# Norms of q and k: from a token-wise product with reductions to ones products on squares of the slot-wise q and k

## The chip, the cores and the metric

The kernel runs on one core of one Trainium2 chip. The metric is the device time of one execution in microseconds (us); its median over several runs is compared. PE is the matrix engine (TensorE), DVE is VectorE, ACT is ScalarE, POOL is GpSimd, and SP issues most DMAs.

## The reference, cut to what matters

The layer is attention, mixture of experts, a small local attention and the experts again, each on a layer norm and with a residual. The change lies in the first part and in the hand-over from it to the first expert unit.

```python
q = split_heads(tokens @ Wq, 16)            # 8 batches, 16 heads, 256 tokens, 16 wide
k, v = kv[..., :16], kv[..., 16:]           # v is 64 wide
q, k, v = l2norm(q), l2norm(k), l2norm(v)
attn = jnp.square(jax.nn.relu(jnp.einsum('bhid,bhjd->bhij', q, k)))
out = tanh_norm(jnp.einsum('bhij,bhjd->bhid', attn, v))
x = x + out @ Wout
x = x + ffn(_layernorm(x))                  # 32 experts, top 8, and a shared one
```

The norms of q and k are not applied to q and k. Scores are taken unnormalised; the factor 1/|k|^2 goes with 1/|v| into v, and 1/|q|^2 goes into the factors of the output.

## The kernel before, in words

Each engine runs a list of instructions in the order in which it is written, and semaphores tie the lists together. Three banks of PSUM (5, 6 and 7) are given out in turns by a table (`attention_turns`); a job waits until the job three turns ahead of it has freed its bank.

**A pass over batch b.** The attention works in 32 steps: 8 batches b of 4 groups g of 4 heads. For each step PE makes scores (`score`, PS<-qk, 8 matmuls), ACT takes their relu in two halves (L583, rl), DVE multiplies scores and relu in two halves (L896, aT), PE multiplies by v (`attend`, PS<-aT,v), and ACT copies and squares the output (L590 and L593). Into these steps are written the products for the next batch n = b+1 and the late work of q = b-1 and r = b-2. A product is written as three matmuls of a high and a low part (`split3`):

- `pairs(n, t)`: q and k of all heads by token (PS<-wah,xTh and two more, 128x512). It serves the norms alone. ACT squares it (L570, sqqk), DVE sums over 16 columns (L880), takes a floor (L886) and a reciprocal (L888, rr).
- `group(n, j)`: q and k again, laid out in slots of 32 rows for the scores, six matmuls of 128x256 (PS<-xTh,wah and so on). A slot holds the q of a head in one half and zeros in the other. Slots j=0 and j=2 hold q, j=1 holds k.
- `values(n, t, k)`: v by token, three matmuls of 128x512 each.
- `norms(q)`: sums over the squares of the attention output by a matmul with ones in the right rows (PS<-sqO,ind, 8 matmuls into four sets of 32 output partitions); `keep_norms` (ACT, n2T), `transpose_norms` (PE) and `gather_norms` (DVE, n2o) bring them to tokens.

**POOL in a pass.** `inverse_deviation` (L409, L411), then for q the root of the output norms (L438, sr, a power) and its product (L442), then for each half of n's tokens a power (L425, vi), a product (L428) and the scaling of v (L434). `attend` of the next batch waits for the last of these.

**Weights of the experts.** 32 pieces of 128x196 come through six stages (wfs). ACT makes the high part (L613), DVE the low part (L941), and piece k may be loaded when the low part of piece k-6 is done. ACT takes 4 pieces a batch, in batches 0 to 7, one at the end of each step. The same SP queue issues these loads and, behind them, the expert weights of tokens (L361 writes them to memory, L375 spreads them into wbc).

**Hand-over.** Unit u=0 of the experts has 17 pairs p (gate and up product on PE, SiLU on ACT, L1115 and L1120 on DVE, high part on ACT, low part on POOL, down product on PE). The end of the attention of batches 6 and 7 is written between its pairs: `spread_factors` (PS<-FT,sel), `norms`, `project`, `output_factors` (L908 to L924), `scale_output` (L931).

## Time and profile before

| | |
|---|---|
| median of 3 runs | 548.19 us (547.99 to 548.92) |
| the profiled execution, its own time | 546.98 us, span 545.2 us |
| PE busy | 526.1 us (96% of the span) |
| DVE, ACT, POOL busy | 421.7, 371.2, 332.5 us |
| first expert product on PE | 214.83 us |

The durations of the trace come from the profiled execution; its time is 1.21 us below the median. The matmuls' ends are modelled and overlap in the trace (a 128x512 matmul is shown with 0.39 us and the next starts 0.23 us later), so work on PE is read from start to start, not from the durations.

### The profile page before, as it was taken

The page shows a single profiled execution, that of the slowest core. Times are in us where ns is not written, and L with a number is a line of the kernel's source. Part 1 is how long each engine was busy: PE and PEld are TensorE (multiplying, and loading weights), DVE is VectorE, ACT ScalarE, POOL GpSimd, SP SyncE. Part 2 cuts the span into 40 slices and gives each one's busy share as a digit, 9 for nine tenths or more (in the row PEclk, how much of TensorE's full clock was granted, in tenths as well). Part 3 has the DMA queues.
Part 4 walks back from the last instruction along what each step waited for, and adds up shares of the span by engine and source line. Part 5 has one row for each costly group of instructions (what it writes and reads, how often), then busy time and mean ns, then how long its engine had stood idle before and what let it go on. Part 6 is the DMA issues. An engine that isn't in the chain of part 4 may idle for free.

```text
span 545.2 us, 10298 instructions
## 1 busy us (share of the span) xinstructions
PE 526.1 (96%) x3322; PEld 394.0 (72%) x3322; DVE 421.7 (77%) x1004; ACT 371.2 (68%) x682; POOL 332.5 (61%) x282
## 2 busy tenths in 40 slices
PE   7899899999999999998999999999999999999997
PEld 6565667676666666776778778778778877788884
DVE  5877888788979687669679679779778778777765
ACT  5697877686778876654555965965965965755654
POOL 6754938475865664484566656656655655666562
PEclk9999999999999999999999999999999999999999
DMA  7401010101010100850490940850860870761930
GB/s 222 131 2 31 1 32 1 32 0 32 1 31 1 31 2 21 189 122 1 107 208 7 222 116 5 207 132 6 197 141 7 194 163 5 181 149 42 220 74 20
DMA packets 37254, 44.77 MB, mean 82 GB/s; under 512 B 5840, under 2 KB 20304, under 8 KB 37200
## 3 DMA queue, kind: packets, MB, share of 16 engines
q1 hardware_dynamic: 32512, 42.40, 33.3%
q10 hardware_dynamic: 4688, 1.71, 1.3%
q8 instruction: 27, 0.44, 0.4%
q14 instruction: 27, 0.22, 0.2%
HBM read 40.94 MB, written 3.15 MB: 81 GB/s over the span
## 4 chain that ended last, share of the span: by engine, by line
PE 29%; POOL 12%; issue 9%; DVE 1%; DMA 1%; ACT 0%; POOLq 0%; DVEq 0%; SPq 0%; ACTq 0%
PE PS L1247 28%; POOL hl L519 10%; DMA wbc<-w_dram 1%; POOL mrstd L510 1%; POOL rstd L463 1%; DVE OTs L931 0%; PE PS L1534 0%; PE PS L1368 0%; DVE PS L1115 0%; DVE wsel L991 0%; POOL fxl L470 0%; PE PS L1555 0%; DVE hb L1120 0%; POOL mve L507 0%; DVE hl L1233 0%
## 5 line engine op out<-in xcount | busy, mean ns | idle before, releaser
L519 POOL TENSOR_TENSOR hl<-hb,hh 128x512 fp32r<-128x512 f32 x127 | 164.5, 1296 | 128.7 <-ACT hh L737 125.5
L730 ACT ACTIVATE sil<-PS 128x512 f32<-128x512 f32 (+1 forms) x136 | 80.8, 595 | 78.8 <-PE PS L1247 77.6
L1115 DVE TENSOR_TENSOR PS<-sil,PS 128x512 f32<-128x512 f32 x128 | 88.3, 690 | 53.0 <-PE PS L1247 32.3
L1247 PE MATMUL PS<-fxh,wfh 128*128 128x512 f32 x264 | 105.1, 398 | 2.5 <-DVE hb L1120 2.5
L737 ACT ACTIVATE hh<-hb 128x512 fp32r<-128x512 f32 x128 | 80.3, 627 | 35.1 <-DVE hb L1120 34.3
L1247 PE MATMUL PS<-fxl,wfh 128*128 128x512 f32 x264 | 104.2, 395 | 0.0
L1247 PE MATMUL PS<-fxh,wfl 128*128 128x512 f32 x264 | 103.8, 393 | 0.0
L1120 DVE TENSOR_TENSOR hb<-PS,wbc 128x512 f32<-128x512 f32 x128 | 88.5, 691 | 13.7 <-DMA wbc<-w_dram 6.4
L896 DVE SCALAR_TENSOR_TENSOR aT<-PS,rl 128x1024 f32<-128x1024 f32 x64 | 75.2, 1217 | 15.0 <-ACT rl L583 14.7
L583 ACT ACTIVATE rl<-PS 128x1024 f32<-128x1024 f32 x64 | 62.9, 1051 | 18.7 <-PE PS L1247 18.7
L438 POOL TENSOR_TENSOR sr<-n2o,half 128x32 f32<-128x32 f32 x7 | 37.9, 5413 | 44.3 <-DVE n2o L903 44.3
L1247 PE MATMUL PS<-aT,v 128*64 128x256 f32 x512 | 62.3, 385 | 0.6 <-POOL v L434 0.6
L1247 PEld LDWEIGHTS PS<-fxh,wfh 128*128 128x128 f32 x264 | 49.6, 188 | 15.8 <-DVE hb L1120 3.4
L1247 PEld LDWEIGHTS PS<-fxh,wfl 128*128 128x128 f32 x264 | 49.6, 188 | 11.9
L1247 PEld LDWEIGHTS PS<-fxl,wfh 128*128 128x128 f32 x264 | 49.6, 188 | 11.4
L1247 PE MATMUL PS<-hh,wfh 128*128 128x512 f32 x128 | 54.2, 424 | 1.0 <-DVE hl L1233 0.6
L1247 PE MATMUL PS<-hh,wfl 128*128 128x512 f32 x128 | 50.6, 396 | 0.0
L1247 PE MATMUL PS<-hl,wfh 128*128 128x512 f32 x128 | 50.5, 394 | 0.0
L1247 PEld LDWEIGHTS PS<-aT,v 128*64 128x64 f32 x512 | 34.0, 136 | 22.6 <-issue 5.6
L425 POOL TENSOR_TENSOR vi<-nm,half 128x16 f32<-128x16 f32 x14 | 40.5, 2894 | 9.8 <-DVE rr L888 9.8
L1247 PE MATMUL PS<-qk 32*128 32x256 f32 x512 | 37.5, 398 | 4.0 <-DVE aT L896 3.3
L1247 PEld LDWEIGHTS PS<-qk 32*128 32x128 f32 x512 | 24.4, 184 | 11.2 <-issue 7.1
(186 smaller groups left out, 899.6 us busy)
## 6 DMA issues: line engine op xcount, KB each, us to landing
wbc<-w_dram SPq DMA_DIRECT2D x48, 512.0 KB, 11.5
wbc<-w_dram SPq DMA_DIRECT2D x32, 128.0 KB, 3.0
wbc<-w_dram SPq DMA_DIRECT2D x16, 256.0 KB, 4.2
wfs<-wf_dram SPq DMA_DIRECT2D x32, 98.0 KB, 2.3
band_dram<-zero SPq DMA_DIRECT2D x16, 80.0 KB, 1.7
band<-band_dram ACTq DMA_DIRECT2D x4, 320.0 KB, 3.0
X<-x_dram SPq DMA_DIRECT2D x1, 896.0 KB, 8.0
Osb<-wa_dram SPq DMA_DIRECT2D x3, 256.0 KB, 3.8
```

What stands on the lines that cost most here:

```text
L425: g.tensor_tensor(vi[:, t, :], nm[:, n % 3, t, 2 * H:3 * H], half[:, 1:2].to_broadcast([P, H]), ALU.pow).then_inc(A("vi"), 1)
L438: g.tensor_tensor(sr[:, :, :], n2o[:, :, :], half[:, 0:1].unsqueeze(2).to_broadcast([P, 2, H]), ALU.pow).then_inc(A("sr"), 1)
L463: g.tensor_tensor(rstd[:, :], ve[:, :], half[:, 1:2].to_broadcast([P, CT]), ALU.pow).then_inc(F("p_rstd"), 1)
L510: g.tensor_tensor(mrstd[:, :], mve[:, :], half[:, 1:2].to_broadcast([P, CT]), ALU.pow).then_inc(M("m_rstd"), 1)
L519: g.tensor_tensor(hl[:, n % RING, :], hb[:, n % RING, :], hh[:, n % RING, :].bitcast(F32), ALU.subtract).then_inc(F("hl"), 1)
L583: s.activation(rl[:, f, :, :], PS[:, S0 + 2 * f:S0 + 2 * f + 2, :], ACT.Relu).then_inc(A("relu"), 1)
L730: s.activation(sil[0:rows, n % 2, :], PS[0:rows, G0 + n % 2, :], ACT.Silu).then_inc(F("silu"), 1)
L737: s.activation(hh[:, n % RING, :], hb[:, n % RING, :], ACT.Copy).then_inc(F("hh"), 1)
L896: v_.scalar_tensor_tensor(aT[:, i % 2, 2 * f:2 * f + 2, :], PS[:, S0 + 2 * f:S0 + 2 * f + 2, :], 0.0, rl[:, f, :, :], ALU.max, ALU.mult).t ...
L1115: v_.tensor_tensor(PS[:, bank, :], sil[:, n % 2, :], PS[:, bank, :], ALU.mult).then_inc(F("t"), 1)
L1120: v_.tensor_tensor(hb[:, n % RING, :], PS[:, bank, :], wbc[u % 2][:, p, :], ALU.mult).then_inc(F("h"), 1)
L1247: return nc.tensor.matmul(o, w, m, start=start, stop=stop)
```

## The change

The token-wise product of q and k (`pairs`), its squares and its reductions go, and with them 512 columns of `wa`. In their place:

- POOL adds the two halves of each q slot (zeros in one of them) and squares the sum (`square_queries`, two adds and two products of 128x256 a batch); ACT squares the k slots (`square_keys`, 128x512). For batch 0 DVE does both.
- PE sums over 16 rows by four matmuls with ones (`pair_sums`, PS<-sqq,indp and PS<-sqk,indp, 128x256 in, 32 partitions out), added into the bank in which the sums of the output squares (`output_sums`) already lie. One copy, one transposition and one reciprocal for both halves then serve q, k and output. `qk` is held twice.
- The order in a pass is new: the three `group` products come first, then `output_sums`, and the four `values` products come in two pairs.
- In batch 0 the second scores are written in halves (`score_half`), and fewer idle-filling transpositions stand there (4 and 4 for 6 and 10).
- Weight pieces: 8 stages, taken by the table `PIECES_IN_SLOTS` (none in batches 0 and 7, 4 in 1 and 6, 6 in 2 to 5).
- ACT runs a SiLU on one column at the very start, and the loads at the start are cut differently (`in_x1`, `in_wq0`, `in_wq1`).
- In unit 0 of the experts the late attention work of batch 7 stands one to two pairs earlier.

```diff
-FIRST_WEIGHTS = (("in_wv0", slice(W_V, W_V + 512)), ("in_wv1", slice(W_V + 512, WA)), ("in_wp", slice(W_QK, W_V)),
-                 ("in_wq", slice(0, W_QK)))
+FIRST_WEIGHTS = (("in_wv0", slice(W_V, W_V + 512)), ("in_wv1", slice(W_V + 512, WA)), ("in_wq0", slice(0, 4 * P)),
+                 ("in_wq1", slice(4 * P, W_V)))
...
-STAGES = 6
+STAGES = 8
 PC = WF // PIECES
+
+PIECES_IN_SLOTS = ((0, 0, 0, 0), (1, 1, 1, 1), (1, 2, 1, 2), (1, 2, 1, 2), (1, 2, 1, 2), (1, 2, 1, 2), (1, 1, 1, 1), (0, 0, 0, 0))
...
+            def square_queries(n, k):
+                pool.wait_ge(*freed("g", n, 2 * k))
+                pool.wait_ge(*full("nb", n - 1))
+                g.tensor_tensor(qs[:, k, :], qk[:, n % 2, 2 * k, 0:L], qk[:, n % 2, 2 * k, L:2 * L], ALU.add).then_inc(A("qs"), 1)
+                pool.wait_ge(A("qs"), 2 * n + k + 1)
+                g.tensor_tensor(sqq[:, k, :], qs[:, k, :], qs[:, k, :], ALU.mult).then_inc(A("sqq"), 1)
...
-                    if u == 0 and p == 5:
+                    if u == 0 and p == 3:
                         last_output_norms(1)
-                    if u == 0 and p == 6:
+                    if u == 0 and p == 4:
                         last_output_scales()
...
+            act.wait_ge(cs("half"), 2)
+            s.activation(unread[:, :], half[:, 0:1], ACT.Silu)
...
-            def square_pairs(n, t):
-                act.wait_ge(*full("qk", n, t))
-                after(act, A("n2q"), 2 * (n - 1) + t + 1)
-                s.activation(sqqk[:, t, :], PS[:, bank_of("qk", n, t), :], ACT.Square).then_inc(free_of("qk", n, t), 1)
...
+            def square_keys(n):
+                act.wait_ge(*freed("g", n, 1))
+                act.wait_ge(*full("nb", n - 1))
+                s.activation(sqk[:, :], qk[:, n % 2, 1, :], ACT.Square).then_inc(A("sqk"), 1)
...
-                relu(NG * b + 1)
+                relu_half(NG * b + 1, 0)
+                if more:
+                    keep_group(n, 0)
+                relu_half(NG * b + 1, 1)
...
-                    square_pairs(n, 0)
-                    square_pairs(n, 1)
+                    keep_group(n, 2)
+                    keep_group(n, 1)
+                    square_keys(n)
                 keep_output(NG * b)
...
+                relu_half(NG * b + 2, 0)
+                if more:
+                    keep_norms(n)
+                relu_half(NG * b + 2, 1)
...
-            def pair_norms(n, t):
-                dve.wait_ge(*freed("qk", n, t))
-                v_.tensor_reduce(n2[:, n % 3, t, 0:2 * H, 0], sqqk[:, t, :].rearrange("p (h d) -> p h d", d=DK),
-                                 AX.X, ALU.add).then_inc(A("n2q"), 1)
...
+            def pair_norms(n):
+                dve.wait_ge(*full("nt", n))
+                sums = PS[:, bank_of("nt", n), 0:2 * P].rearrange("p (i c x) -> p i c x", i=2, c=NG)
+                v_.tensor_scalar(nm[:, :, :].rearrange("p i (c x) -> p i c x", c=NG), sums[:, :, :, HG:3 * HG],
+                                 NORM_EPS * NORM_EPS, None, ALU.max).then_inc(free_of("nt", n), 1)
+                dve.wait_ge(*freed("nt", n))
+                v_.reciprocal(rr[:, n % 3, :, :], nm[:, :, :]).then_inc(A("rr"), 1)
...
-                        if p == 8:
+                        if p == 6:
                             output_factors(B - 1)
-                        if p == 12:
+                        if p == 11:
                             scale_output(B - 1, 0)
...
+            def pair_sums(n):
+                if n < 2:
+                    bank, done = turn("nb", n)
+                else:
+                    bank, done = turns.at["nb", n][0], full("nb", n)[0]
+                pe.wait_ge(A("sqq"), 2 * (n + 1))
+                pe.wait_ge(A("sqk"), n + 1)
+                pe.wait_ge(cs("indp"), 2 * HG)
+                for c in range(NG):
+                    squared = sqq[:, c, :] if c < 2 else sqk[:, (c - 2) * L:(c - 1) * L]
+                    last = mm(PS[SLOT * c:SLOT * (c + 1), bank, 0:L], indp[:, :], squared, n < 2, True)
                 last.then_inc(done, 1)
...
                     pe.wait_ge(*freed("xT", n))
-                    pairs(n, 0)
-                    pairs(n, 1)
+                    for j in (0, 2, 1):
+                        group(n, j)
+                if b:
+                    output_sums(n)
                 attend(NG * b)
+
+                score(NG * b + 2)
                 if more:
+                    pair_sums(n)
                     values(n, 0, 0)
                     values(n, 0, 1)
-                if b:
-                    norms(q)
-
-                score(NG * b + 2)
-                if more:
-                    values(n, 1, 0)
-                if b:
-                    transpose_norms(q)
-                if more:
-                    values(n, 1, 1)
+                transpose_norms(n)
                 attend(NG * b + 1)
...
-                        if p == 16:
+                        if p == 15:
                             project(B - 1, 0)
                             project(B - 1, 1)
```

**PE, the front of the pass over batch 3.** Before, from the end of the old factors to the first attend: six matmuls of the token-wise product (wah,xTh and so on; FT,sel are the factors of batch 1).

```order
L1247 MATMUL PS<-FT,sel 128x256 x4
L1247 MATMUL PS<-wah,xTh 128x512
L1247 MATMUL PS<-wal,xTh 128x512
L1247 MATMUL PS<-wah,xTl 128x512
L1247 MATMUL PS<-wah,xTh 128x512
L1247 MATMUL PS<-wal,xTh 128x512
L1247 MATMUL PS<-wah,xTl 128x512
L1247 MATMUL PS<-aT,v 64x256 x8
```

Now, from the last of the 18 slot matmuls of batch 4 (xTh,wal) to its first values: sqO,ind are the sums of the output squares, sqq,indp and sqk,indp the new ones products.

```order
L1317 MATMUL PS<-xTh,wal 128x256
L1317 MATMUL PS<-sqO,ind 32x256 x8
L1317 MATMUL PS<-aT,v 64x256 x8
L1317 MATMUL PS<-qk 128x256 x8
L1317 MATMUL PS<-sqq,indp 32x256 x2
L1317 MATMUL PS<-sqk,indp 32x256 x2
L1317 MATMUL PS<-wah,xTh 128x512
```

The six 512-column matmuls are gone, all slot products and the output sums stand ahead of the first attend, and four ones matmuls stand behind the second scores.

**POOL, a whole pass (batch 2).** Before, from the inverse deviation to the scaling of the second half of v:

```order
L409 TENSOR_SCALAR veA<-mvA 128x2
L411 TENSOR_TENSOR rsA<-veA,half 128x2
L438 TENSOR_TENSOR sr<-n2o,half 128x32
L442 TENSOR_TENSOR nn<-sr,rr 128x32
L425 TENSOR_TENSOR vi<-nm,half 128x16
L428 TENSOR_TENSOR vc<-vi,rr 128x16
L434 TENSOR_TENSOR v<-v,vc 128x1024
```

Now, up to the same product for the first half of v:

```order
L467 TENSOR_TENSOR qs<-qk 128x256
L469 TENSOR_TENSOR sqq<-qs 128x256
L441 TENSOR_SCALAR veA<-mvA 128x2
L443 TENSOR_TENSOR rsA<-veA,half 128x2
L467 TENSOR_TENSOR qs<-qk 128x256
L469 TENSOR_TENSOR sqq<-qs 128x256
L479 TENSOR_TENSOR sr<-n2o,half 128x32
L483 TENSOR_TENSOR nn<-sr,rr 128x32
L458 TENSOR_TENSOR vi<-nv,half 128x16
```

Four operations of 128x256 stand ahead of the root of the output norms, one pair on each side of the inverse deviation.

**ACT, the first two steps of the pass over batch 3.** Before:

```order
L583 ACTIVATE rl<-PS 128x1024 x2
L570 ACTIVATE sqqk<-PS 128x512 x2
L590 ACTIVATE Osb<-PS 128x512
L593 ACTIVATE sqO<-PS 128x512
L558 ACTIVATE v<-PS 128x512 x2
L599 ACTIVATE n2T<-PS 128x256
L613 ACTIVATE wfh<-wfs 128x196
```

Now:

```order
L627 ACTIVATE rl<-PS 128x1024
L617 ACTIVATE qk<-PS 128x512
L627 ACTIVATE rl<-PS 128x1024
L617 ACTIVATE qk<-PS 128x512 x2
L622 ACTIVATE sqk<-qk 128x512
L639 ACTIVATE Osb<-PS 128x512
L642 ACTIVATE sqO<-PS 128x512
L662 ACTIVATE wfh<-wfs 128x196
L627 ACTIVATE rl<-PS 128x1024
L648 ACTIVATE n2T<-PS 128x256
L627 ACTIVATE rl<-PS 128x1024
```

The copies of the slots moved to the front, one of them between the two relu halves, and the copy of the sums stands between the next two.

## Rows read from the trace of the kernel before

**Rows 1.** Two stretches: start:end, length, then PE, PEld, DVE, ACT, POOL busy, clock, DMA

```profile
92.60:118.50 25.90, 25.66 (x227) 17.62 (x226) 21.02 (x40) 19.95 (x35) 16.51 (x11) 1.00 0.08 17
...
215.00:265.00 50.00, 45.98 (x258) 35.84 (x257) 37.72 (x97) 25.17 (x50) 29.41 (x24) 1.00 0.41 92
```

**Rows 2.** PE in order of time, batch 3: start us, us, what

```profile
94.55 0.47 PE L1247 MATMUL PS<-wah,xTh 128*128 128x512 f32 x1
...
96.12 1.95 PE L1247 MATMUL PS<-aT,v 128*64 128x256 f32 x16
98.00 0.50 PE L1247 MATMUL PS<-wah,xTh 128*128 128x512 f32 x1
...
99.58 1.07 PE L1247 MATMUL PS<-sqO,ind 128*32 128x256 f32 x16
100.58 1.15 PE L1247 MATMUL PS<-qk 32*128 32x256 f32 x16
...
103.69 1.95 PE L1247 MATMUL PS<-aT,v 128*64 128x256 f32 x16
...
108.63 0.39 PE L1247 MATMUL PS<-xTh,wah 128*128 128x256 f32 x1
...
110.26 1.95 PE L1247 MATMUL PS<-aT,v 128*64 128x256 f32 x16
112.14 0.39 PE L1247 MATMUL PS<-xTh,wah 128*128 128x256 f32 x1
...
113.05 1.15 PE L1247 MATMUL PS<-qk 32*128 32x256 f32 x16
```

**Rows 3.** POOL in order of time, batches 0, 2 and 3

```profile
20.37 2.84 POOL L434 TENSOR_TENSOR v<-v,vc 128x1024 f32<-128x1024 f32 x1
...
77.44 5.41 POOL L438 TENSOR_TENSOR sr<-n2o,half 128x32 f32<-128x32 f32 x1 [5.75 <-DVE n2o L903]
...
91.55 1.90 POOL L434 TENSOR_TENSOR v<-v,vc 128x1024 f32<-128x1024 f32 x1
96.58 0.22 POOL L409 TENSOR_SCALAR veA<-mvA 128x2 f32<-128x2 f32 x1 [3.13 <-DVE mvA L856]
96.89 0.71 POOL L411 TENSOR_TENSOR rsA<-veA,half 128x2 f32<-128x2 f32 x1
103.38 5.41 POOL L438 TENSOR_TENSOR sr<-n2o,half 128x32 f32<-128x32 f32 x1 [5.78 <-DVE n2o L903]
```

**Rows 4.** The page's row of POOL's commonest group

```profile
L519 POOL TENSOR_TENSOR hl<-hb,hh 128x512 fp32r<-128x512 f32 x127 | 164.5, 1296 | 128.7 <-ACT hh L737 125.5
```

**Rows 5.** PE in order of time, batch 0 and the start of batch 1

```profile
23.26 1.95 PE L1247 MATMUL PS<-aT,v 128*64 128x256 f32 x16 [0.59 <-POOL v L434]
...
41.91 1.15 PE L1247 MATMUL PS<-qk 32*128 32x256 f32 x16 [0.53 <-DVE aT L896]
```

**Rows 6.** PE in order of time, the hand-over to the experts

```profile
217.74 0.51 PE L1247 MATMUL PS<-FT,sel 32*128 32x256 f32 x4 [1.27 <-ACT FT L605]
...
223.22 0.50 PE L1247 MATMUL PS<-fxh,wfh 128*128 128x512 f32 x1 [1.08 <-DVE hb L1120]
...
247.85 0.50 PE L1247 MATMUL PS<-fxh,wfh 128*128 128x512 f32 x1 [1.42 <-DVE hb L1120]
```

**Rows 7.** ACT and the SP queue in order of time, same place

```profile
216.29 0.37 ACT L613 ACTIVATE wfh<-wfs 128x196 fp32r<-128x196 f32 x1 [4.09 <-DMA wfs<-wf_dram]
...
218.93 1.28 ACT L730 ACT_TABLE_LOAD   x1
...
215.10 1.82 SPq L361 DMA_DIRECT2D w_dram<-wTs  x4
```

**Rows 8.** DVE in order of time: batch 2, hand-over, first expert unit

```profile
88.95 0.18 DVE L922 CAST Fpad<-ff 128x32 fp32r<-128x32 f32 x1
...
221.48 0.36 DVE L941 TENSOR_TENSOR wfl<-wfs,wfh 128x196 fp32r<-128x196 f32 x1
...
244.30 1.16 DVE L922 CAST Fpad<-ff 128x32 fp32r<-128x32 f32 x1
```

More of the change, by code:

```diff
@@ L139, in expert_turns, with pieces_in @@
             turns.add(MB, "pc", u + 1)
+def pieces_in(b, slots=range(NG)):
+    first = sum(sum(PIECES_IN_SLOTS[c]) for c in range(b))
+    a = first + sum(PIECES_IN_SLOTS[b][:slots[0]])
+    return range(a, a + sum(PIECES_IN_SLOTS[b][k] for k in slots))
 def up_banks():
@@ L323, in pair, with by_group, by_groups, query_norms @@
             return u * NP + p
+        def by_group(a, t):
+            return a[:, t, :].rearrange("p (c m) -> p c m", c=NG)
+        def by_groups(a):
+            return a.rearrange("p i (c m) -> p i c m", c=NG)
+        def query_norms(q):
+            return by_groups(rr[:, q % 3, :, 0:H])
+        def key_norms(n, t):
+            return rr[:, n % 3, t, H:2 * H].rearrange("p (c m) -> p c m", c=NG)
+        def outputs_summed(q):
+            return (A("nbo"), q + 1) if q + 2 < B else full("nb", q + 2)
+        def gathered(q):
+            return (A("n2o"), q + 1) if q + 2 < B else freed("nt", q + 2)
         def low_of(n):
@@ L704, in _ @@
                     tanh_norms(q)
-                weight_high(NG * b + 2)
+                if more:
+                    square_values(n, 1)
+                for k in pieces_in(b, [2]):
+                    weight_high(k)
+                if last:
+                    prep_normalise(1, range(CT // 2, CT))
                 relu(NG * b + 4)
@@ L1069, in _ @@
                     mask_scores(0)
-                if b:
-                    if not last:
-                        for k in range(NG * q, NG * b):
-                            weight_low(k)
+                if b and more:
+                    for k in pieces_in(q, [0, 1]):
+                        weight_low(k)
+                if last:
                     gather_norms(q)
@@ L1103, in _ @@
                 if last:
[L1104 removed]
+                    for k in pieces_in(q):
                         weight_low(k)
@@ L1276, in values @@
                 by_token(n, t, W_V + 512 * k, bank).then_inc(done, 1)
-            def pairs(n, t):
-                bank, done = turn("qk", n, t)
-                by_token(n, t, W_QK, bank).then_inc(done, 1)
             def group(n, j):
@@ L1318, in attend, with output_sums @@
                 last.then_inc(A("av"), 1)
-            def norms(q):
-                pe.wait_ge(A("sqO"), NG * (q + 1))
-                bank, done = turn("nb", q)
+            def output_sums(n):
+                pe.wait_ge(A("sqO"), NG * (n - 1))
+                bank, done = turn("nb", n)
                 for s in range(2):
@@ L1325, in norms, with transpose_norms @@
                         last = mm(PS[SLOT * g:SLOT * (g + 1), bank, 0:L], ind[:, s, :], sqO[:, g, s * L:(s + 1) * L],
-                                  s == 0, s == 1)
+                                  s == 0, s == 1 and n >= B)
+                last.then_inc(A("nbo") if n < B else done, 1)
+            def pair_sums(n):
+                if n < 2:
+                    bank, done = turn("nb", n)
+                else:
[6 more added lines that the diff above has]
+                    last = mm(PS[SLOT * c:SLOT * (c + 1), bank, 0:L], indp[:, :], squared, n < 2, True)
                 last.then_inc(done, 1)
-            def transpose_norms(q):
-                pe.wait_ge(*freed("nb", q))
-                bank, done = turn("nt", q)
+            def transpose_norms(n):
+                pe.wait_ge(*freed("nb", n))
+                bank, done = turn("nt", n)
                 for it in range(2):
@@ L1407, in _ @@
             pe.wait_ge(cs("wpl"), 1)
-            pairs(0, 0)
-            pairs(0, 1)
-            pe.wait_ge(cs("wpl"), 2)
             group(0, 0)
             group(0, 1)
-            fill_idle(6, "g", 0, 2)
+            pe.wait_ge(cs("wpl"), 2)
+            group(0, 2)
+            fill_idle(4, "xT", 1)
             score(0)
-            for j in range(2, NQ):
-                group(0, j)
             transpose_tokens(1)
+            pair_sums(0)
+            transpose_norms(0)
             pe.wait_ge(cs("ind"), 4)
@@ L1458, in _ @@
                 if more:
-                    group(n, 0)
-                    group(n, 1)
+                    values(n, 1, 0)
+                    values(n, 1, 1)
                 attend(NG * b + 2)
-                if more:
-                    group(n, 2)
+                if r >= 0 and more:
+                    project(r, 0)
                 if last_batch:
```

280 lines of the change are left out of this document (154 added, 126 removed).

## The prediction

> **What bounds the kernel now.** I read the busy time by stretch first. In a full pass over a batch PE is busy 25.66 of 25.90 us at clock 1.00, while DVE has 21.02, ACT 19.95 and POOL 16.51 [rows 1]. So a pass ends when PE has done its work, and PE's time line shows that work without a gap [rows 2]. From 215 to 265 us, the hand-over to the experts, PE is busy only 45.98 of 50.00 us [rows 1]; its gaps there are 1.27, 1.08 and 1.42 us, behind the factors and behind DVE [rows 6]. The rest of the experts is not touched. The gain must come from PE's work in the passes and from these gaps; a new wait would have to come from POOL, ACT or DVE.
>
> **The steady passes, batches 2 to 6.** What PE loses is the token-wise product: from its first matmul at 94.55 to attend at 96.12, 1.57 us [rows 2]. What it gains is four ones matmuls. The same form with eight takes 99.58 to 100.58, 1.00 us, so four take 0.50 (below 0.50 nothing speaks for it, above it 0.6 if starting costs as much for four). The slot products stood in two runs of 12 and 6 matmuls, 108.63 to 110.26 and 112.14 to 113.05, 1.63 + 0.91 = 2.54 us [rows 2]. From the two, six more matmuls cost 0.72, so one run of 18 costs 1.63 + 0.72 = 2.35: 0.19 less. The values of the second half stood alone, around the transposition: from the scores at 100.58 to attend at 103.69 are 3.11 us; now it is scores 1.1, one pair of values 1.58 (98.00 to 99.58) and the transposition of about 0.3: 2.98, 0.13 less [rows 2]. Sum: 1.57 - 0.50 + 0.19 + 0.13 = 1.39 a pass. Everything else PE does is the same, only moved. I take 1.3, since the first slot product now asks for three freed banks within 2.35 us where the token-wise product asked for two. Five passes: **6.5**.
>
> **What hides the rest of a pass.** ACT gives up two squares of 128x512 and gets one, and takes up to six weight pieces for four: 19.95 stays about 20 of the 24.5 us that are left. DVE gives up two sums over 512 columns and one reciprocal and gets two more weight pieces: about 20.5 of 24.5. The relu half behind the first slot copy comes later, by about 1 us; PE asks for its result only after the slot products, the output sums and attend, which now take 2.35 + 1.00 + 1.88 (96.12 to 98.00) [rows 2], some 5.2 us from the end of the factors. So it is covered, by about 1 us. If it were not, the whole excess would be PE's.
>
> **POOL is the close one.** Its chain from the root of the output norms to the last scaling of v is 77.44 to 91.55 + 1.90, 16.0 us; the inverse deviation is 96.58 to 96.89 + 0.71, 1.0 us [rows 3]. New are four operations of 128x256. The nearest row has twice the columns and 1.296 us [rows 4]; half of it is 0.65, with the gaps 3.0 us for all four. Before the next root come the ones product and the way back over ACT, PE and DVE: before, 99.58 [rows 2] to 103.38 [rows 3], 3.8 us, less 0.5 for the shorter product, 3.3. The ring is 16.0 + 1.0 + 3.0 + 3.3 = 23.3 us, against PE's 25.9 - 1.4 = 24.5. PE stays the bound with 1.2 us to spare.
>
> In the first row of POOL the scaling of v took 2.84 us beside DVE's two-input operation and 1.90 otherwise [rows 3], and a cast on DVE took 1.16 us for 0.18 while POOL was at work [rows 8]. The Trainium skill says why ("SBUF — State Buffer", SBUF: two separate sides): DVE and GpSimd share a port pair that a GpSimd operation, or a DVE operation with two SBUF inputs, holds for its whole length while the other is blocked. By that rule, which these rows agree with, the new squares would meet DVE's weight pieces and both would stretch; it speaks against moving work to POOL. Stretched as the scaling was, by 1.5, the four operations cost 1.3 us more and the ring is 24.6: about level with PE.
>
> **Batch 0 and the start.** The first attend at 23.26 waits 0.59 us for POOL's scaling of v, which started at 20.37 [rows 5, 3]. Its inputs wait for sums that now come by way of PE and ACT, so I let the earlier scores bring nothing here. From 23.26 to the first scores of batch 1 at 41.91 are 18.65 us. The work behind it is now four attends of 1.88, three scores of 1.1, two pairs of values of 1.58, the ones product 0.5, transpositions 0.7, the filler 1.0: 16.1 us. But POOL's squares start only when the scaling has ended (23.2) and with the inverse deviation between them take 4.0 us, to 27.2, where PE is ready for the ones product at 23.26 + 1.88 + 1.1 = 26.2: 1.0 us of waiting. 18.65 - 17.1 = **1.5** (nothing if the scaling itself is 1.5 us later, 3 if the start moves forward too). In batch 1 the same wait returns, since POOL is still behind: I take **0.7** of the 1.4 (bounds 0 and 1.4).
>
> **The hand-over.** ACT waits 4.09 us for the next-to-last weight piece and does the factors' copy only behind it; PE waits 1.27 us for that copy [rows 7, 6]. No piece is left for batch 7, so this gap goes: 1.3. The SP queue issues the token weights at 215.10 behind those loads [rows 7]; now it can at once. The table load of 1.28 us [rows 7] goes from there too, and so does the weight piece of 0.36 us ahead of the first expert product on DVE [rows 8]. Of the 1.08 us gap I take 0.3 off; the factors of both group pairs stand between and remain. The third gap, 1.42 us at 247.85, lies where the output factors and the choice of groups stand behind the same pair p=8 on DVE, with casts stretched to 1.16 us [rows 6, 8]. The factors stand at p=6 now; I take the whole gap. Sum 1.3 + 0.3 + 1.4 = **3.0** (bounds 1.3, if only the first goes, and 3.8).
>
> The Trainium skill ("ScalarE: Activation LUTs", What ACT_TABLE_LOAD costs) gives 1283 ns for the load and about as much again for draining. The trace agrees with the load and shows no second part here.
>
> **Sum.** 6.5 + 0.7 + 1.5 + 3.0 = 11.7 us. The profiled execution would go from 546.98 to 535.3, and the median, 1.21 above it, from 548.19 to **536.5**.
>
> **The rivals.**
> 1. *POOL becomes the bound* (0.15). The four operations cost as much as those of 128x512, 1.3 each, 2.6 more in all: ring 25.9, the passes gain nothing, and about 4.5 remain: 543.7. With a stretch by 1.5 and some more waiting it is 538 to 541. For it: the stretched rows. Against: 1.2 us to spare, and few two-input operations on DVE in that part of the pass.
> 2. *The hand-over's gaps only move* (0.12). DVE's chain of two operations for each pair and the two or three banks of the up product leave little room, so a block at p=6 costs PE as one at p=8 did. Then 1.3 for 3.0: 538.2.
> 3. *Slower than before* (0.03). One mechanism: PE waits at the ones product for POOL's squares in each pass. Start and hand-over bring 4.5, so six passes must each be 0.8 longer than now, the ring 26.7, which asks 1.6 us for each of the four operations, above the 1.296 us of twice the columns. At 2.0 us each the ring is 28.7 and the time about 560.
> 4. *The gains are larger* (0.1). The start moves forward by 1.5 more and the passes reach 1.5: 533.5.
>
> **How the numbers follow.** The forecast as worked out, 534.5 to 539, has 0.6. Rivals 1 and 2 with their ends reach 544, rival 4 532. Leaving out the 2 in 10 at the ends gives 532.5 to 541. Within 0.2% (1.1 us), about what a measurement of this kernel can tell from no change, lies only a thin part of rival 1: 0.03. Slower 0.03, faster 0.94.
>
> **What would show it.** In the new trace: passes of 24.6 us from scores to scores for batches 2 to 6; ones products that begin right behind the second scores except in batches 0 and 1; squares on POOL of about 0.65 us; the first expert matmul about 8.7 us earlier, near 206; no wait of ACT for weights and a PE gap below 0.3 us at the factors. Wrong it would be by waits of PE for POOL at the ones product, or by a gap of over 1 us around p=7 of unit 0.

## The result and the profile after

The changed kernel takes **541.7 us** (median of 5 runs, 541.04 to 542.08) against 548.92 of the kernel before beside it (547.99 to 550.62): a ratio of **0.987** (95% interval 0.985 to 0.9889). Forecast were 536.5, in a range of 532.5 to 541.0. The sign and the order of the gain are right; 5.2 us of the forecast are missing, and the time lies 0.7 us above the range.

| | before | after |
|---|---|---|
| profiled execution, its own time | 546.98 us | 541.96 us |
| span | 545.2 us | 539.8 us |
| PE, POOL busy | 526.1, 332.5 us | 519.2, 349.7 us |
| scores of batch 1 begin | 41.91 us | 44.20 us |
| first expert product | 214.83 us | 210.26 us |

The trace of before stems from an execution 1.9 us below the median of this comparison, so its span gives 5.4 us of the gain where the medians give 7.2. The sums below are made between the traces.

**A steady pass.** Busy time by stretch, columns as in [rows 1], from the first factors (FT) of batch 4 to those of batch 5:

```profile
116.37:140.87 24.50, 24.40 (x230) 16.92 (x229) 22.02 (x48) 20.40 (x36) 19.18 (x15) 1.00 0.10 26
```

The pass is 24.50 us and PE is busy in all but 0.1 of it. The new squares on POOL, in order of time (batch 4 here), lie ahead of the root of the output norms:

```profile
118.16 1.91 POOL L475 TENSOR_TENSOR v<-v,vc 128x1024 f32<-128x1024 f32 x1
120.02 0.74 POOL L467 TENSOR_TENSOR qs<-qk 128x256 f32<-128x256 f32 x1
120.84 0.61 POOL L469 TENSOR_TENSOR sqq<-qs 128x256 f32<-128x256 f32 x1
...
122.42 0.73 POOL L467 TENSOR_TENSOR qs<-qk 128x256 f32<-128x256 f32 x1
123.23 0.61 POOL L469 TENSOR_TENSOR sqq<-qs 128x256 f32<-128x256 f32 x1
128.53 5.43 POOL L479 TENSOR_TENSOR sr<-n2o,half 128x32 f32<-128x32 f32 x1 [4.69 <-DVE n2o L982]
```

0.74 and 0.61 us each: the 0.65 that was taken. POOL still waits 4.69 us for DVE ahead of the root.

**PE's waits** in order of time; the number in brackets is the idle time ahead of the row:

```profile
16.41 0.41 PE L1317 MATMUL PS<-sqq,indp 128*32 128x256 f32 x2 [1.62 <-issue]
...
17.54 0.44 PE L1423 MATMUL PS<-ident,n2T 128*128 128x128 f32 x2 [0.49 <-ACT n2T L648]
19.71 1.09 PE L1486 MATMUL PS<-ident 128*128 128x128 f32 x4 [1.74 <-DVE xTl L928]
...
44.20 1.15 PE L1317 MATMUL PS<-qk 32*128 32x256 f32 x16 [1.41 <-DVE aT L973]
...
66.54 1.10 PE L1317 MATMUL PS<-qk 32*128 32x256 f32 x13 [0.84 <-DVE aT L973]
68.74 0.50 PE L1317 MATMUL PS<-FT,sel 32*128 32x256 f32 x4 [0.84 <-DVE OTs L1009]
...
150.36 0.41 PE L1317 MATMUL PS<-sqq,indp 128*32 128x256 f32 x2 [1.18 <-POOL sqq L469]
...
217.05 0.50 PE L1317 MATMUL PS<-fxh,wfh 128*128 128x512 f32 x1 [0.80 <-DVE hb L1191]
...
236.85 0.50 PE L1317 MATMUL PS<-fxh,wfh 128*128 128x512 f32 x1 [0.72 <-DVE hb L1191]
...
325.64 0.33 PE L1476 MATMUL PS<-ident,comb 128*128 128x128 f32 x1 [0.86 <-DVE comb L1076]
```

In the passes, the ones products wait only in batch 5. Of the three gaps of [rows 6] the first is gone and the others are 0.80 and 0.72 us. New are three gaps within 5 us at the start, one ahead of batch 1, and one at the combination of the weights (comb), deep in the experts. What the gaps at the start bring with them is seen in the busy time by stretch. First the kernel before:

```profile
13.00:20.00 7.00, 5.24 (x52) 4.28 (x51) 6.82 (x15) 4.75 (x8) 6.29 (x4) 1.00 0.73 197
```

and the changed kernel:

```profile
13.00:20.00 7.00, 3.15 (x34) 1.73 (x32) 6.86 (x15) 3.85 (x6) 5.85 (x4) 0.93 0.70 194
20.00:24.00 4.00, 4.00 (x26) 2.90 (x24) 1.66 (x6) 1.02 (x1) 2.69 (x1) 0.50 0.43 129
24.00:28.00 4.00, 4.00 (x30) 3.35 (x29) 2.79 (x3) 3.23 (x5) 2.71 (x5) 0.78 0.00 0
```

PE is busy 3.15 of 7 us where it was busy 5.24, and then its granted clock is 0.50, the 1.2 GHz level, for 4 us in which it has work all the time.

**Where the 11.7 us went**, between the two traces:

| stretch | forecast | measured |
|---|---|---|
| start and batch 0, to batch 1's scores | -1.5 | **+2.3** (41.91 to 44.20) |
| batch 1, to the first factors of batch 2 | -0.7 | -1.6 |
| batches 2 to 6 | -6.5 | -5.75 |
| batch 7 and unit 0, to the next unit's tokens (xnp) | -3.0 | -2.6 |
| the experts from there on | 0 | **+2.2** |

A second trace of the kernel before (e5) has batch 1's scores at 42.29 us and 60.43 us from the first transposition of comb to the next unit's tokens, where the first has 41.91 and 59.92, so a row can be half a microsecond off by chance.

### The profile page after: what moved, and what is told of

It reads as the page before. It is cut to its first block, busy times and chain, and to the rows that moved or that the text cites. A ratio compares the mean times of both kernels' runs of the same rounds, so it can differ in the third digit from the quotient of the medians.

```text
span 539.8 us, 10360 instructions
## 1 busy us (share of the span) xinstructions
PE 519.2 (96%) x3334; PEld 389.9 (72%) x3334; DVE 417.8 (77%) x1001; ACT 370.3 (69%) x675; POOL 349.7 (65%) x311
## 3 DMA queue, kind: packets, MB, share of 16 engines
HBM read 40.68 MB, written 3.15 MB: 81 GB/s over the span
## 4 chain that ended last, share of the span: by engine, by line
PE 45%; POOL 30%; issue 18%; DVE 5%; ACT 2%; POOLq 0%; DVEq 0%; ACTq 0%
PE PS L1317 44%; POOL hl L564 14%; POOL vi L458 4%; POOL sr L479 4%; POOL v L475 1%; POOL qs L467 1%; POOL rstd L504 1%; POOL sqq L469 1%; DVE aT L973 1%; POOL mrstd L555 1%; POOL rsA L443 1%; DVE n L944 1%; DVE PS L1186 0%; DVE hb L1191 0%; ACT sqv L612 0%
## 5 line engine op out<-in xcount | busy, mean ns | idle before, releaser
L458 POOL TENSOR_TENSOR vi<-nv,half 128x16 f32<-128x16 f32 x14 | 40.6, 2897 | 7.8 <-DVE nv L947 7.8
```

Source lines behind the costliest of these rows:

```text
L458: g.tensor_tensor(vi[:, t, :], nv[:, n % 2, t, :], half[:, 1:2].to_broadcast([P, H]), ALU.pow).then_inc(A("vi"), 1)
```

## The experiments

All but the kernel before itself are edits of the changed kernel. Kernels under one letter and number range (1 to 4, 5 to 8, 9 to 12, f, g) ran on one chip. The level of before was 547.77, 548.67, 548.63, 548.64 and 548.29 us.

| run | us | ratio to before (95%) |
|---|---|---|
| e1 changed kernel | 542.02 | 0.9902 (0.9873 to 0.9932) |
| e2 filler at the start | 540.16 | 0.9862 (0.9842 to 0.9881) |
| e3 deviation moved | 540.29 | 0.9863 (0.9847 to 0.9879) |
| e4 both | 538.15 | 0.9824 (0.9804 to 0.9844) |
| e5 before | 548.63 | one run |
| e6 combination first | 539.69 | 0.9838 (0.9814 to 0.9863) |
| e7 filler and square of v | 537.92 | 0.981 (0.9786 to 0.9834) |
| e8 six more on POOL | 557.06 | 1.0166 (1.0132 to 1.0201) |
| e9 old weight pieces | 541.44 | 0.9872 (0.9857 to 0.9888) |
| e10 late work as before | 542.76 | 0.9894 (0.9876 to 0.9912) |
| e11 norms alone | 543.0 | 0.9896 (0.9875 to 0.9916) |
| e12 all mended | 536.63 | 0.9785 (0.9761 to 0.9809) |
| f1 changed kernel | 541.64 | 0.9877 (0.9859 to 0.9895) |
| f2 norms alone | 544.24 | 0.9927 (0.9909 to 0.9945) |
| f3 combination first | 540.77 | 0.9862 (0.9843 to 0.9882) |
| f4 norms alone, combination first | 542.37 | 0.9882 (0.9861 to 0.9902) |
| g1 all mended | 536.04 | 0.9776 (0.9752 to 0.9801) |
| g2 all mended, more filler | 535.84 | 0.9768 (0.9742 to 0.9795) |

### The start and batch 5: e1 to e4

```diff
             transpose_tokens(1)
+            keep_busy(12)
             pair_sums(0)
+            keep_busy(4)
             transpose_norms(0)
+            keep_busy(14)
```

```diff
                     square_queries(b + 1, 1)
+                if b == B - 3:
+                    prep_deviation(0)
...
-                if b == B - 4:
-                    prep_deviation(0)
```

> The changed kernel unaltered, as the level for the others of this group. Every theory: 541.7 us (541.0 to 542.1), batch 1's scores at 44.2 us. If its experts, whose code the change leaves alone but for unit 0, take the same time as in the first trace, the 2.3 us that they lost is a lasting property; if they give them back, it was chance.

> The changed kernel with 30 idle-filling transpositions of 128x128 in the three places at the start where PE idles (12 ahead of the first ones product, 4 ahead of the transposition of its sums, 14 behind). The data waits stay as they are. Theory A (the granted clock): the start loses its time because PE is idle for 1.6, 0.5 and 1.7 us within 5 us and then runs at the lower clock from 20 to 25 us; with the filler the clock stays up, the 16 score matmuls take 1.15 us for 2.10, and batch 1's scores start 2.5 to 3 us earlier, at about 41.5; 538.7 to 539.5 us in all. Rival B (the data): the values of the first half are scaled late by POOL, the clock is only a side effect; batch 1 starts at 44.2 as before and the time stays at 541.7. Rival C: the filler itself is in the way and the time rises by up to 1 us.

> The changed kernel with one POOL operation pair (the deviation for the first expert unit) moved from the end of batch 4 to behind the second squares of batch 5. Theory A: the 1.18 us that PE waited for POOL's squares at the ones product of batch 5 go, the pass of batch 5 takes 24.5 us for 25.75, and the whole 1.0 to 1.2 us less, 540.6. Rival (POOL's ring is the bound there): the work only moves within the ring, PE waits as long in batch 5 or in batch 6 and the time stays at 541.7. Third: the time gained is lost again in the experts, whose pace hangs on where POOL and DVE meet; then the first expert product comes 1.2 us earlier and the end does not.

> Both edits together. Theory A: the gains add, 2.7 plus 1.1 us, 537.9 us. Rival: the experts' pace hangs on the phase in which they are entered, so that the parts do not add; then the first expert product is 3.8 us earlier and the end anything from 1.5 to 5 us.

**e2: the clock.** PE in order of time, with the filler:

```profile
16.35 0.41 PE L1317 MATMUL PS<-sqq,indp 128*32 128x256 f32 x2 [0.30 <-issue]
...
17.48 0.44 PE L1423 MATMUL PS<-ident,n2T 128*128 128x128 f32 x2
...
19.66 0.63 PE L1486 MATMUL PS<-ident 128*128 128x128 f32 x4 [0.21 <-DVE xTl L928]
20.21 1.16 PE L1317 MATMUL PS<-qk 32*128 32x256 f32 x16
...
41.72 1.15 PE L1317 MATMUL PS<-qk 32*128 32x256 f32 x16 [1.42 <-DVE aT L973]
```

The ones product, the transposition and the last filler begin at the same moment as before the edit (16.35, 17.48, 19.66 against 16.41, 17.54, 19.71): what PE waits for has not moved. The clock is 1.00 from 13 to 28 us, and batch 1's scores come at 41.72 against 44.20, 43.29 and 44.12 in the three traces of the unedited kernel (in the second the clock from 20 to 24 us was 0.63, not 0.50). So the fallen clock cost 1.6 to 2.5 us, and the data did not: A holds, B falls. The median is 1.9 us below that of e1, which leaves it 0.7 us above the range that A gave. The fall stood in all twelve traces of kernels without this filler and in none of the six with it. The wait of 1.41 us ahead of batch 1 has another cause, as e7 shows.

**e3: batch 5.** The 1.18 us are gone. From the first factors of batch 5 to those of batch 6 are 141.54 to 166.04, 24.50 us, against 25.75. The operations that stood ahead of the squares (the deviation for the experts, L501 to L507, 144.53 to 146.42) make up this wait; moved behind the squares they cost nothing. The median is 1.7 us lower on the same chip, where the wait explains 1.2, and e4 shows that both edits add: 3.9.

### POOL's slack: e8

```diff
             for b in range(B):
+                if b:
+                    for _ in range(6):
+                        dose()
                 if b + 1 < B:
                     square_queries(b + 1, 0)
```

Here `dose` is one product of 128x128, written to a tile that nothing reads.

> The changed kernel with six more products of 128x128 on POOL in each batch from 1 on, ahead of the squares (work added only, 0.35 to 0.45 us each, some 2.4 us a batch). Theory A: in a steady pass POOL's squares end 0.77 us ahead of the ones product, so that is POOL's slack; PE waits there 1.6 us a pass (2.8 in the pass over batch 5, where 1.18 are waited already), and the six passes from 1 to 6 are 9 to 11 us longer: 551 to 553 us. Rival B (the slack is the 1.2 us of the prediction): 1.2 us a pass, 549. Rival C (POOL is no matter before the root of the output norms, where it idles for 4.7 us): the ones product waits, but the pass ends as before; 542 to 544.

Busy time by stretch in e8, the passes over batches 3 and 4:

```profile
96.91:123.23 26.32, 24.45 (x235) 16.94 (x230) 21.15 (x41) 20.61 (x36) 21.47 (x21) 1.00 0.10 25
123.23:151.13 27.90, 26.00 (x235) 17.84 (x230) 22.32 (x49) 20.83 (x36) 22.11 (x22) 0.94 0.09 23
```

The added products took 3.07 us a batch (99.73 to 102.80), not the 2.4 expected, and the pass over batch 3 became 1.82 us longer. The ring of POOL is thus 26.32 - 3.07 = **23.25 us** without them, and its slack 1.25 us: rival B with the prediction's own 1.2 (it gave 23.3), not the 0.77 us by which the squares end ahead of the ones product (99.34 against 100.11). The difference lies on the way from the ones product back to the root, which took 3.45 us here (106.64 to 110.09) and 3.92 in the unedited kernel (100.11 to 104.03). The largest wait comes in batch 1:

```profile
53.53 0.41 PE L1329 MATMUL PS<-sqq,indp 128*32 128x256 f32 x2 [2.62 <-POOL sqq L470]
```

Behind it, and behind the waits of 1.79 and 3.06 us in batches 4 and 5, the clock fell, to 0.94 on the mean of each of the three passes. The pass over batch 4 is 1.6 us longer than that over batch 3, although its wait is the same but for 0.03 us. So the total of 15 us is above all three expectations, and it is not the same in each pass: against the changed kernel the passes over batches 1 to 5 are 4.2, 1.2, 1.8, 3.4 and 3.5 us longer, and that over batch 6 not at all (25.25 us in both).

### Batch 1's wait: e7

```diff
                     keep_values(n, 1, 1)
+                if b == 0:
+                    square_values(n, 1)
                 keep_output(NG * b + 2)
...
-                if more:
+                if more and b:
                     square_values(n, 1)
```

> The changed kernel with the filler of the second run (batch 1's scores at 41.7 us with it) and, in batch 0, ACT's square of the second half of v ahead of the copies of the third output instead of behind them. Theory A: PE's wait of 1.42 us ahead of batch 1's scores comes from DVE, which waits 2.13 us for that square and does the products for the scores only behind it; with the square 1.4 us earlier the wait falls to 0.2 to 0.6 us and batch 1's scores start at about 40.7; 1 us less than with the filler alone. Rival B (POOL): the scaling of v ends no earlier, and the attention product of batch 1 then waits for it; no gain. Rival C (ACT): the copies of the output come 1 us later, and the wait moves to the scores before.

DVE in order of time, the changed kernel ahead of batch 1:

```profile
40.36 1.22 DVE L944 TENSOR_REDUCE n<-sqv 128x16 f32<-128x1024 f32 x1 [2.13 <-ACT sqv L612]
41.61 0.19 DVE L947 TENSOR_REDUCE nv<-n 128x16 f32<-128x32 f32 x1
41.71 2.35 DVE L973 SCALAR_TENSOR_TENSOR aT<-PS,rl 128x1024 f32<-128x1024 f32 x2
```

and in e7, where all is earlier by the filler too:

```profile
36.60 1.22 DVE L946 TENSOR_REDUCE n<-sqv 128x16 f32<-128x1024 f32 x1 [0.68 <-ACT sqv L612]
...
38.49 2.36 DVE L975 SCALAR_TENSOR_TENSOR aT<-PS,rl 128x1024 f32<-128x1024 f32 x2 [0.44 <-ACT rl L627]
```

PE's wait falls from 1.42 to 0.38 us, within the 0.2 to 0.6 expected, and batch 1's scores begin at 40.99 us (41.72 in e2, 40.7 expected). A holds: the second half of v comes later in the new order, ACT squares it behind the output's copies, and DVE stands still for it with the products for the scores queued behind.

### The experts: e5 and e6

```diff
-                        if p == 10:
-                            mix_halo(u - 2)
                         if p == 12:
                             add_mix(u - 2)
...
                             combine(u + 1)
+                    if p == 10 and 2 <= u < NC + 2:
+                        mix_halo(u - 2)
```

> The kernel before once more, for a second trace of it. It tells how much of the experts' time is chance. If its expert units take the same again (39.05 us from the third to the fourth transposition of combined weights, 201.5 from the third to the last) and those of the changed kernel 40.1 to 40.4 in each of five traces, the first 1.2 us lost there are a lasting property; if it shows 40.2 too, they are chance.

> The changed kernel with one DVE copy (32x256, bs) put behind the combination of the weights instead of ahead of it, in expert units 2 to 5. The combination (comb, 128x128, two inputs in SBUF) then starts 0.33 us earlier, at 0.45 us ahead of POOL's next subtraction instead of within 0.1 us of it. Theory A (DVE is shut out while POOL's operation runs, 1.19 us for 0.29, and PE waits 0.86 us): the stretched comb and the wait of PE go, about 1.2 us less from the third to the fourth transposition of combined weights, 540.5 us. Rival B (the loss comes from elsewhere and comb only shows it): comb takes 0.29 us but PE or DVE waits as long within the next two pairs; 541.7. Rival C: the copy, put later, meets POOL or is late for PE, and the loss moves there.

DVE and POOL of the changed kernel in order of time (third expert unit):

```profile
323.87 0.16 DVE L1071 RECIPROCAL winv<-ws 128x4 f32<-128x4 f32 x1
324.40 1.19 DVE L1076 SCALAR_TENSOR_TENSOR comb<-winv,wsel 128x128 f32<-128x128 f32 x1 [0.37 <-DVE winv L1071]
...
324.16 1.28 POOL L564 TENSOR_TENSOR hl<-hb,hh 128x512 fp32r<-128x512 f32 x1 [0.76 <-ACT hh L792]
```

The same place in the second trace of before (e5):

```profile
333.39 0.29 DVE L998 SCALAR_TENSOR_TENSOR comb<-winv,wsel 128x128 f32<-128x128 f32 x1
...
333.49 1.34 POOL L519 TENSOR_TENSOR hl<-hb,hh 128x512 fp32r<-128x512 f32 x1 [0.77 <-ACT hh L737]
```

and in e6:

```profile
323.22 0.29 DVE L1076 SCALAR_TENSOR_TENSOR comb<-winv,wsel 128x128 f32<-128x128 f32 x1
323.58 0.41 DVE L1242 COPY bs<-PS 32x256 f32<-32x256 f32 x1
...
323.64 1.28 POOL L564 TENSOR_TENSOR hl<-hb,hh 128x512 fp32r<-128x512 f32 x1 [0.77 <-ACT hh L792]
```

Before, DVE's operation starts 0.10 us ahead of POOL's and takes 0.29 us; in the changed kernel it is recorded 0.24 us behind POOL's start and ends only about when POOL's does, at 325.5 us. That is the stretch that the prediction weighed for the squares ([rows 3, 8] and the rule behind them), at a place that nobody had touched. Yet DVE is ready equally early in both kernels: the reciprocal ahead of comb (winv) starts 0.29 to 0.30 us before POOL's operation. The stretch stood in every trace of the changed kernels that leave this order (12 of 12) and in neither of the two of before. The distance from the third to the fourth transposition of comb on PE is 39.95 to 40.37 us in those twelve. It is 39.05 in the first trace of before, and 38.89 to 39.29 in the six with the combination first: 1.2 us for the stretch. The second trace of before has 40.14 without the stretch; PE waited 0.70 us for ACT's SiLU there, so part of the distance is chance. In the median, e6 gains 2.3 us against e1 on another chip and f3 0.9 against f1 on the same; A's 1.2 lies between.

The rest of the experts, from the fourth to the last transposition of comb, takes 162.1 to 164.9 us in kernels with the same code there (the two traces of before: 162.4, 162.1; the three of the changed kernel: 163.4, 164.9, 162.3). The first trace of the changed kernel is 1.0 us above that of before, which is within this spread.

### The hand-over and its parts: e9 to e11, f1 to f4

e9 takes the weight pieces by the old table (`STAGES = 6`, four a batch), e10 puts the late work back:

```diff
-                        if p == 6:
+                        if p == 8:
                             output_factors(B - 1)
-                        if p == 11:
+                        if p == 12:
                             scale_output(B - 1, 0)
...
```

e11 and f2 undo both and the SiLU at the start, f4 has the combination first as well.

> The changed kernel with the weight pieces as before (six stages, four a batch in batches 0 to 7, the last low part on DVE at the experts' start). Theory A (the prediction's hand-over): ACT waits again for the next-to-last piece and PE 1.3 us for the factors (FT), DVE has the extra piece ahead of the first expert product; the marks behind unit 0 come 1.3 to 1.6 us later than in the changed kernel, the first expert product and the passes stay. 543.0 to 543.5 us. Rival B (the gap went because the attention is ahead of its loads or because the order around it changed): no wait at FT, 541.7. Rival C: DVE and ACT have fewer pieces in batches 2 to 5, so passes get no slower but batch 0 and 7 do.

> The changed kernel with the late attention work of batch 7 at the pairs of unit 0 where it stood before. Theory A (the prediction's third gap): PE waits 1.4 us again near pair 8, where output factors and choice of groups meet on DVE; the second expert unit starts 1.2 to 1.5 us later, 543.1 us. Rival B (the gaps only move, the place is no matter): the same sum of PE gaps from 205 to 262 us as in the changed kernel, 1.5 us, and 541.7.

> The new norms alone: weight pieces, the late work in unit 0 and the absent SiLU at the start as in the kernel before. Theory A: passes and start as in the changed kernel, hand-over as before, so 3.0 us (2.6 to 3.4) more at the start of the second expert unit than the changed kernel, 544.7 us. Rival B (the parts overlap): only 1.5 to 2.5 us more, since one wait covers another. If comb in the third unit takes 0.29 us here, the stretch in the changed kernel comes from the hand-over's new timing; if 1.2, from the new passes or from chance.

> The changed kernel unaltered, as the level for this group: 541.7 to 542.0 us. The combination of the third unit takes 1.19 us as in each trace so far.

> The new norms with the weight pieces, the late work in unit 0 and the start of ACT as in the kernel before. Theory A (what is gained by unit 1 stays): 3.0 us above the changed kernel of this group, 544.9. Rival B (the experts give about half of it back, since a late entry meets POOL and DVE at other moments): 1 to 2 us above it, 543.3.

> The changed kernel with the combination ahead of the copy in units 2 to 5. Theory A (the stretched combination costs 1.2 us and is the only lasting loss of the experts): 1.2 us (0.8 to 1.8) below the changed kernel of this group, 540.6. Rival B (chance meetings of the engines in the experts make up for it): within 0.5 us of it.

> The norms alone, with the combination first. Theory A: the parts add, 3.0 us above the changed kernel with the combination first and 1.2 us below the norms alone, 543.7. Rival B: less than 2 us above the former.

From the first transposition of comb to the tokens of the next unit (ident,xnp) on PE are 56.88 us in the changed kernel (206.15 to 263.03) and 59.92 in the one before (210.71 to 270.63; 60.43 in its second trace). With the old pieces they are 58.41: PE's gap at FT is back, and the second gap is 1.08 us again, for 0.80 in the changed kernel,

```profile
213.04 0.50 PE L1318 MATMUL PS<-FT,sel 32*128 32x256 f32 x4 [1.18 <-ACT FT L654]
...
218.55 0.50 PE L1318 MATMUL PS<-fxh,wfh 128*128 128x512 f32 x1 [1.08 <-DVE hb L1191]
```

and with the late work as before 58.11, with the third gap of [rows 6] back in place,

```profile
242.33 0.50 PE L1317 MATMUL PS<-fxh,wfh 128*128 128x512 f32 x1 [1.43 <-DVE hb L1191]
```

1.5 and 1.2 us. With both and the table load it is 3.15 us in e11 (60.03) and 2.8 and 2.7 in f2 and f4 (59.68, 59.58). In e11 the second gap was 1.41 us where f2 has 1.09, so the table load's move shows no gain of its own: 1.5 and 1.2 make up the 2.7 to 2.8. By the traces A holds for e9, e10 and e11. At the end less of it is left. Where the old pieces are back, some 0.3 us is given back by the next unit already. In the medians on one chip the norms alone are 2.6 us above the changed kernel (f2 and f1), and 1.6 with the combination first in both (f4 and f3), where A said 3.0 for each. The second is what B said (less than 2), the first lies between A and B (1 to 2); each median is known to about 1 us either way, so these pairs don't decide. The traces of f2 and f4 also have a fall of the clock in batch 2 that those of f1 and f3 have not (below), which is no part of the hand-over. e9's median of 541.44 shows nothing of its 1.5 us: its trace takes 202.8 us from the third to the last transposition of comb, where the three of the unedited kernel take 203.8 on the mean. A step of 1 us is not told from medians of four runs on different chips.

### All together: e12, g1, g2

> The changed kernel with all four edits: filler at the start, the square of v earlier in batch 0, the deviation behind the squares, comb ahead of the copy. Theory A: the gains add: 2.4 (fill) + 0.8 (square) + 1.0 (deviation) + 1.2 (comb) = 5.4 us, 536.3 us. Rival B: what is won in the first stretch is lost to chance meetings of POOL, DVE and ACT in the experts; the second expert unit starts 4.2 us earlier but the end lies anywhere from 536 to 539.

> The four edits together once more, as the level for the next: 536.6 us. Its last trace had the clock at 0.63 from 66 to 70 us and lost some 1.3 us there; if this one shows 1.00, the same kernel goes both ways.

> The same with 18 filling transpositions for 10 ahead of the early scores of batch 2, so that PE's wait of 0.84 us there is filled. Theory A (PE's idle spells let the clock fall): the clock stays at 1.00 from 60 to 90 us, from batch 2's first factors to those of batch 3 are 24.5 us, and the time is 0 to 1.3 us below the one above, 535.5 to 536.5. Rival B (the fall comes from something else, or the next wait of 0.84 us is enough for it): the clock falls in some traces all the same and the time is as above. Rival C: the filler ends too late and delays the scores by up to 0.3 us.

The four edits together take 536.6 and 536.0 us, **5.4 to 5.6 us less** than the changed kernel (5.4 expected, A), and 0.9776 (0.9752 to 0.9801) of the kernel before. e12 lost 1.3 us at one place, which g1, the same kernel, did not. Busy time by stretch, e12 and then g1, 66 to 70 us:

```profile
66.00:70.00 4.00, 4.00 (x26) 3.61 (x28) 3.54 (x9) 2.01 (x4) 3.46 (x5) 0.63 0.00 0
```

```profile
66.00:70.00 4.00, 3.95 (x40) 3.12 (x42) 3.90 (x8) 2.93 (x5) 3.74 (x6) 1.00 0.00 0
```

Six of the seventeen traces of changed kernels that have these waits (all but g2) show this fall of the clock at the start of batch 2, behind PE's waits of about 0.41, 0.84 and 0.84 us, and a pass 1.3 to 1.5 us longer (e3, e10, e11, e12, f2, f4); neither trace of before has it, with waits of 0.76 and 0.84 us. g2 fills the first of the 0.84 us; its clock stays at 1.00 and its median of 535.84 is 0.2 us below g1's, which tells nothing, since g1's clock did not fall either. Whether the filler prevents the fall stays open.

## Why the prediction was right, and where it failed

- **The bound and the steady passes** were right: 24.50 us for 24.6 forecast; ones products of 0.5 us behind the second scores; squares of 0.74 and 0.61 us for 0.65. Undisturbed passes (batches 2 to 4) each gained 1.42 to 1.44 us, a little more than the 1.3 taken. The sum of five passes was 5.75 us and not 6.5. 1.18 us are the wait in batch 5: the prediction counted the squares and the inverse deviation in POOL's ring, but not the deviation for the experts, which stands ahead of the squares in one pass and takes 1.9 us, where the squares had ended 0.77 us ahead of PE.
- **POOL's ring** was right in its size: 23.3 us estimated, 23.25 worked out of e8. That they agree so closely is partly luck: POOL's own work was 20.0 us forecast and 19.8 measured, but the way from the ones product back to the root, set at 3.3, takes 3.92 us in the changed kernel and 3.45 where POOL is the bound. The squares were not stretched by DVE (0.73 to 0.75 and 0.61 to 0.62 us in every batch). Rival 1 is out.
- **Batch 0 and the start** is the step that failed: "I let the earlier scores bring nothing here", 1.5 us of gain, with a loss excluded by the bounds (0 to 3). It went 2.3 us the other way. The first attend, left at 23.26 in the sum, came at 26.43, 3.2 us later; from there to batch 1's scores were 17.77 us for 17.1 forecast and 18.65 before. In place of the forecast the runs showed two things that a sum of work can't hold. Before, scores, slot products and ten fillers lay from 15 to 20 us and PE was busy 5.24 of the 7 us from 13 to 20, at clock 1.00. In the changed kernel the slot products were done by 13 us and the first scores by 14.4, ahead of data that came hardly earlier (xTl starts on DVE at 19.21, before at 19.69), so PE stood idle for 3.9 us of 5 and then ran at half clock (1.6 to 2.5 us, e2). The token-wise product is not alone in this: the change also took out 8 of the 16 fillers that stood around these scores, and about 1.5 of the 2.1 us of lost busy time are fillers. No run has the new norms with the old fillers, so it stays open whether the clock would have held with them. And a wait of 1.41 us for 0.53 [rows 5] came up ahead of batch 1, by way of ACT's square and DVE (1.0 us of it mended in e7). With the clock restored batch 1's scores are only 0.2 us earlier than before, and 0.9 with e7's edit: even then not the 1.5 of the forecast. The wait of 1.0 us for POOL that was set down was not there in the changed kernel; with the filler 0.24 us of it appears (the squares end at 26.80, the ones product starts at 26.90 in e2).
- **Batch 1** brought 1.6 us, not 0.7: its wait for POOL was not there either.
- **The hand-over** was right in mechanism and nearly in size: 3.0 forecast, 3.04 measured up to the next unit (3.55 against the second trace of before, 2.7 to 3.15 by putting the parts back); the old weight pieces are worth 1.5 (forecast 1.3 and 0.3, for the gaps at FT and behind it) and the one at 247.85 1.2 (1.4). The cast of [rows 8] is still stretched (1.21 us for 1.16), but at p=6 PE loses 0.72 us by it and not 1.42: "I take the whole gap" was half right. (The rule that the prediction quotes speaks of two SBUF inputs; the cast has one, so its rows are no instance of the rule as quoted.) The gap of 1.08 us fell by 0.28, as set down (0.3); it is back with the old pieces alone (e9), so the table load had no share in it. Batch 7 itself lost 0.5 us. Rival 2 is out in the traces; of the medians one pair gives 2.6 and one 1.6 us, where it says 1.3.
- **"The rest of the experts is not touched"** was right of the code and wrong of the time: 2.2 us more. Some 1.2 of them are a single operation of DVE that POOL now shuts out; the rest is within what the same code varies by.
- The chances: faster, at 0.94, came true; the range missed by 0.7 us, since it held nothing for a slower start or for the experts. The kernel before, too, stood 0.7 us higher in this comparison than in the one that the forecast started from (548.92 for 548.19).

Left open: why comb is stretched in each trace of the changed kernels that keep the order and in neither of before, at the same distance to POOL's operation (it is so with the hand-over as before as well, in e11 and f2); whether the old number of fillers would have held the clock; and the other chance differences of the experts.

## What to carry to other kernels

Work that a change takes off the bounding engine is only a gain where something else is ready: at the start or at a seam, look in the trace for what the removed work was hiding, and price the idle time twice, as itself and as the clock that may fall behind it. When an engine is given more work, list all that it does in each pass, also what it does only once, and measure its slack by adding a known dose. And when two engines shut each other out, an operation with 0.1 us to spare can flip anywhere downstream: order the short one so that it has a margin.

## What the runs showed of the hardware

- PE's granted clock fell to the 1.2 GHz level during or just behind three waits of 1.6, 0.5 and 1.5 to 1.7 us within 5 us, in all twelve traces that have them. It stayed there while PE was busy without a gap for 3 to 6 us, and did not fall in any of the six traces in which 30 transpositions of 128x128 filled most of the same waits. Around waits of about 0.41, 0.84 and 0.84 us within 8.3 us it fell in six of seventeen traces, and in one of two of the same kernel (e12 and g1).
- A DVE operation with two inputs in SBUF of 0.29 us took 1.18 to 1.21 us when a POOL operation of 1.28 us was in the way, in 12 traces, and PE waited 0.84 to 0.89 us behind it; placed 0.42 us ahead of POOL's it took 0.29 in all six. The Trainium skill ("SBUF — State Buffer", SBUF: two separate sides) says that the one that holds the shared port pair blocks the other for its whole length; these numbers agree.
- Six products of 128x128 on POOL took 3.07 us (e8), 0.51 each, while one of 128x256 takes 0.61: with twice the columns only 0.1 us more, so here the size is the smaller part of the time.
